# Attention scores from split queries and keys: three rounded products in place of one full-precision product, gammas moved ahead of the transposition, heads paired, the causal mask by selection

## The reference, cut to what matters

```python
x = _rmsnorm(tokens, norm_w)
q = (x @ Wq).reshape(b, n, QH, DH).transpose(0, 2, 1, 3)       # QH = 16 query heads of DH = 64
kv = x @ Wkv                                                    # H = 8 key and value heads
k = kv[..., :H * DH].reshape(b, n, H, DH).transpose(0, 2, 1, 3)
v = kv[..., H * DH:].reshape(b, n, H, DH).transpose(0, 2, 1, 3)
q = _mh_rmsnorm(q, q_gamma)                                     # l2norm(q) * (gamma + 1) * 8
k = _mh_rmsnorm(k, k_gamma)
q = q.reshape(b, H, g, n, DH)                                   # g = 2 query heads share a key head
sim = jnp.einsum('bhgid,bhjd->bhgij', q, k)
sim = jnp.tanh(sim / SOFTCLAMP) * SOFTCLAMP
sim = sim * DH ** (-0.5)
sim = jnp.where(causal, neg, sim)                               # token i sees tokens j <= i
attn = jax.nn.softmax(sim, axis=-1)
out = jnp.einsum('bhgij,bhjd->bhid', attn, v)                   # summed over g as well
return out.transpose(0, 2, 1, 3).reshape(b, n, H * DH) @ Wout
```

## Time and profile before

| | us |
|---|---|
| median of 3 runs | 2039.68 (2038.79 to 2041.76) |
| the profiled execution, its own time | 2037.89 |
| its span, first to last instruction | 2036.2 |
| PE busy, share of the span | 1841.0, 90% |
| DVE busy | 1184.6, 58% |
| ACT busy | 876.8, 43% |
| POOL busy | 473.1, 23% |

### The profile page before, as it was taken

The page is one execution under the profiler, slowest core; times in us unless marked ns, Lnnn a source line. Parts: engine busy times, 40 slices in busy tenths (PEclk is TensorE's granted clock), DMA queues, the critical chain, the costliest instruction groups (busy, mean ns, idle before and its releaser), DMA issues. The chain is left out here.

```text
span 2036.2 us, 31526 instructions
## 1 busy us (share of the span) xinstructions
PE 1841.0 (90%) x11768; PEld 1585.8 (78%) x11768; DVE 1184.6 (58%) x2083; ACT 876.8 (43%) x1076; POOL 473.1 (23%) x376
## 2 busy tenths in 40 slices
PE   3699999999969989998998999699999999999997
PEld 2698988988957877777787778578778787777876
DVE  6788788888865786776678676323241423414141
ACT  3655654545525764664576466122221222222221
POOL 2100000000022231221232123133433324333342
PEclk8799999999998999998999999799999999999999
DMA  8131222224001002000200100150000000000000
GB/s 168 49 128 49 96 78 90 76 99 143 22 32 63 23 15 77 24 15 9 85 23 15 56 22 22 49 223 14 8 21 0 21 0 21 21 0 21 0 11 12
DMA packets 17240, 96.81 MB, mean 48 GB/s; under 512 B 3270, under 2 KB 3398, under 8 KB 11209
## 3 DMA queue, kind: packets, MB, share of 16 engines
q1 hardware_dynamic: 17100, 94.90, 13.9%
HBM read 82.27 MB, written 24.15 MB: 52 GB/s over the span
## 5 line engine op out<-in xcount | busy, mean ns | idle before, releaser
L556 PE MATMUL conv<-w_hi,x_hi 128*128 128x368 f16 (+5 forms) x1320 | 355.8, 279 | 4.2 <-DVE planes L452 4.2
L556 PE MATMUL conv<-w_lo,x_hi 128*128 128x368 f16 (+5 forms) x1320 | 356.2, 279 | 0.0
L556 PE MATMUL conv<-w_hi,x_lo 128*128 128x368 f16 (+5 forms) x1320 | 355.0, 279 | 0.0
L818 POOL TENSOR_TENSOR probs<-probs,mask 128x512 f32<-128x512 f32 x128 | 166.8, 1303 | 444.1 <-ACT probs L892 444.1
L1310 ACT ACTIVATE raw_c<-ring,sh 128x512 f32<-128x512 f32 x128 | 88.2, 689 | 370.3 <-PE ring L1407 370.3
L1098 PE MATMUL mixed<-v,probs 128*128 128x65 f32 x1536 | 202.9, 283 | 41.5 <-DVE parts L978 41.5
L1098 PEld LDWEIGHTS mixed<-v,probs 128*128 128x128 f32 x1536 | 187.2, 197 | 56.8 <-issue 40.0
L1407 PE MATMUL ring<-ha_hi,wh 128*128 128x512 f32 x512 | 208.2, 407 | 16.9 <-POOL ha_lo L1272 16.9
L1272 POOL TENSOR_TENSOR ha_lo<-raw_c,ha_hi 128x512 fp32r<-128x512 f32 x128 | 165.0, 1289 | 210.1 <-DVE ha_hi L1322 210.1
L1407 PE MATMUL ring<-ha_lo,wh 128*128 128x512 f32 x512 | 205.4, 401 | 0.0
L1322 DVE CAST ha_hi<-raw_c 128x512 fp32r<-128x512 f32 x128 | 80.7, 631 | 212.9 <-ACT raw_c L1310 210.7
(11 more groups left out here) (148 smaller groups left out, 3563.7 us busy)
## 6 DMA issues: line engine op xcount, KB each, us to landing
xt<-x_columns_in SPq DMA_DIRECT2D x12, 1163.0 KB, 5.3
xp<-x_patches_in SPq DMA_DIRECT2D x12, 1152.0 KB, 5.2
hidden_words<-hidden_weights_in SPq DMA_DIRECT2D x8, 1408.0 KB, 8.2
words<-hidden_words SPq DMA_DIRECT2D x32, 352.0 KB, 3.1
wh<-hidden_words SPq DMA_DIRECT2D x2, 4096.0 KB, 21.1
tokens<-planes SPq DMA_DIRECT2D x4, 1024.0 KB, 3.9
lines<-tokens SPq DMA_DIRECT2D x4, 1024.0 KB, 5.4
h<-tokens SPq DMA_DIRECT2D x4, 1024.0 KB, 7.4
```

Source lines behind the costliest of these rows:

```text
L556: ins = pe.matmul(out, xs[:, c, RI - 1 - i:RI - 1 - i + NR, :, x].rearrange("p r g -> p (r g)"), w, start=(t == 0), stop=(t == len(terms) ...
L818: pool.tensor_tensor(diag, diag, both, ALU.mult).then_inc(s_mask, 1)
```

## The change

Queries and keys are each split into a high part, rounded to fp32r (the type in which the kernel's other split products run), and a low part, the rest. Each score product becomes three: high x high, low query x high key, high query x low key, accumulated in PSUM. ACT writes the high part while it copies the bank (`q_hi`, `k_hi`, L888 of the changed kernel), and DVE then subtracts it from the same bank to get the low part (L971), so a bank of transposed data is read by two engines one after the other.

Both gammas are multiplied into the query columns of `raw` ahead of the transposition, on DVE (L966), with `gamma` now 128 x 1024 and loaded so. The heads are regrouped by the host's order of Wq: one score step is now a pair of neighbouring key heads (one on partitions 0 to 63, the other on 64 to 127), with one query head of each. So keys are transposed as they are, once: three transposition jobs per token block in place of four, and `keys` is gone. The two steps of a pair leave their results in `o` (first step) and `parts` (second step), and one addition of 256 columns per pair takes the place of two of 128. POOL masks with two affine selections of 128 x 2 x 128 on `probs` itself in place of a multiplication by a mask tile. The gammas' staging buffer is `xp`, so SP waits with their load until the last split of `xp`.

```diff
-                    for dst, src in ((sh.norm_w, NW), (sh.gq, GQ), (sh.gamma, GK)):
-                        sp.dma_start(dst[:], src).then_inc(sh.s_small, 16)
+                    sp.wait_ge(s_lo, LAST + 2)
+                    for dst, src in ((sh.norm_w[:], NW), (gq, GQ), (sh.gamma[:], GK)):
+                        sp.dma_start(dst, src).then_inc(sh.s_small, 16)
...
-                dve.tensor_tensor(sh.gamma[:], sh.gamma[:], sh.gq[:], ALU.mult).then_inc(sh.s_gamma, 1)
+                dve.tensor_tensor(sh.gamma[:], sh.gamma[:], gq, ALU.mult).then_inc(sh.s_gamma, 1)
...
-    [("make", 11), ("make", 7), ("scale", 1)],
+    [("make", 7), ("scale", 1)],
     [("make", 12)],
-    [("make", 13), ("make", 14), ("make", 15)],
+    [("make", 13), ("make", 14)],
...
-        qt = sb("qt", [P, 2, HEADS, TOK])
-        kt = sb("kt", [P, 2, HEADS, TOK])
+        q_hi = sb("q_hi", [P, 2, HEADS, TOK], F32R)
+        q_lo = sb("q_lo", [P, 2, HEADS, TOK], F32R)
+        k_hi = sb("k_hi", [P, 2, EB, TOK], F32R)
+        k_lo = sb("k_lo", [P, 2, EB, TOK], F32R)
...
-                        pool.tensor_tensor(diag, diag, both, ALU.mult).then_inc(s_mask, 1)
+                        settle(pool, s_settle)
+                        for jb in range(2):
+                            diag = probs[:, n % 4, :, 2 * jb * P:(2 * jb + 1) * P]
+                            ins = pool.affine_select(out=diag, in_=diag, compare_op=ALU.is_ge, fill=0.0, base=0,
+                                                     pattern=[[0, 2], [1, P]], channel_multiplier=-1)
+                        ins.then_inc(s_mask, 1)
...
-                        dve.tensor_tensor(heads[:, 0:QH], heads[:, 0:QH], by[:, 0:QH].to_broadcast([P, QH, DH]), ALU.mult)
-                        for m in range(2):
-                            ins = dve.tensor_tensor(keys[:, tb, :, m], heads[:, QH:],
-                                                    by[:, QH:].to_broadcast([P, HEADS, DH]), ALU.mult)
-                        ins.then_inc(s_qn, 1)
+                        dve.tensor_tensor(heads, heads, by, ALU.mult).then_inc(s_scaled, 1)
+                        dve.wait_ge(s_scaled, image(g, step[1]) * 2 + tb + 1)
+                        dve.tensor_tensor(raw[:, tb, 0:KV], raw[:, tb, 0:KV], gamma[:], ALU.mult).then_inc(s_qn, 1)
...
-                        dve.tensor_tensor(kt[:, img % 2, 4 * r:4 * r + 4, P * tb:P * tb + P], bank, by,
-                                          ALU.mult).then_inc(s_emptied["keys"], 1)
+                        dve.wait_ge(s_qkhi, image(g, img) * 6 + 3 * tb + r + 1)
+                        dve.tensor_tensor(transposed(q_lo, k_lo, img, tb, r), bank,
+                                          transposed(q_hi, k_hi, img, tb, r).bitcast(F32), ALU.subtract)\
+                           .then_inc(s_emptied["queries" if r < 2 else "keys"], 1)
...
-                        dve.tensor_tensor(parts[:], got[:, :, :, 0:DH], rl[:].to_broadcast([P, 2, 2, DH]),
+                        pair = o[:, img % 2, :, 2 * (hd // 2):2 * (hd // 2) + 2]
+                        dve.tensor_tensor(parts[:] if hd % 2 else pair, got[:, :, :, 0:DH], rl[:].to_broadcast([P, 2, 2, DH]),
                                           ALU.mult).then_inc(s_mixread, 1)
-                        dve.wait_ge(s_mixread, g * NH + n + 2)
-                        dve.tensor_tensor(o[:, img % 2, :, hd], parts[:, :, 0], parts[:, :, 1],
-                                          ALU.add).then_inc(s_o, 1)
+                        if hd % 2:
+                            dve.wait_ge(s_mixread, g * NH + n + 2)
+                            dve.tensor_tensor(pair, pair, parts[:], ALU.add).then_inc(s_o, 1)
...
                         for jb in range(2):
-                            for m in range(2):
-                                rows = slice(DH * m, DH * m + DH)
-                                ins = pe.matmul(sim[:, n % 2, m, 2 * P * jb:2 * P * jb + P * (2 - jb)],
-                                                kt[rows, img % 2, hd, P * jb:P * jb + P],
-                                                qt[rows, img % 2, hd, P * jb:TOK], start=True, stop=True)
+                            for t, (k, q) in enumerate(((k_hi, q_hi), (k_hi, q_lo), (k_lo, q_hi))):
+                                for m in range(2):
+                                    rows = slice(DH * m, DH * m + DH)
+                                    ins = pe.matmul(sim[:, n % 2, m, 2 * P * jb:2 * P * jb + P * (2 - jb)],
+                                                    k[rows, img % 2, hd // 2, P * jb:P * jb + P],
+                                                    q[rows, img % 2, hd, P * jb:TOK], start=(t == 0), stop=(t == 2),
+                                                    skip_group_check=True)
```

More of the change, by code:

```diff
@@ L109, in token_stage @@
         xp = sb("xp", [P, XW])
+        gq = xp[:, 0:QH * DH]
         x_hi = sb("x_hi", [P, CHANNELS, NR + 4, GI, NC], F16)
@@ L601, in first_order @@
     order += [("make", 0, j) for j in (4, 5, 6)] + [("scale", 0, 0), ("sum", 0, 1), ("root", 0, 1)]
-    order += [("make", 0, j) for j in (3, 7, 8, 9, 10, 11)] + [("scale", 0, 1)]
-    return order + [("make", 0, j) for j in (12, 13, 14, 15)]
+    order += [("make", 0, j) for j in (3, 7, 8, 9, 10)] + [("scale", 0, 1)]
+    return order + [("make", 0, j) for j in (12, 13, 14)]
 def attention_order(last):
@@ L702, in attention_stage @@
         raw = sb("raw", [P, 2, QK])
-        keys = sb("keys", [P, 2, HEADS, 2, DH])
         rn = sb("rn", [P, 2, QK // DH])
@@ L743, in attention_stage @@
         s_rn = sem("b_rn")
+        s_scaled = sem("b_scaled")
         s_qn = sem("b_qn")
+        s_qkhi = sem("b_qkhi")
         s_score = sem("b_score")
@@ L765, in attention_stage, with transposed @@
         image = lambda g, img: g * GI + img
+        def transposed(q, k, img, tb, r):
+            heads = q[:, img % 2, 4 * r:4 * r + 4] if r < 2 else k[:, img % 2]
+            return heads[:, :, P * tb:P * tb + P]
         @block.sync
@@ L796, in _ @@
             pool.memset(v[:], 1.0).then_inc(s_const, 1)
[L797 to L801, removed]
             def emit(run, g):
@@ L878, in emit @@
                                 act.activation(squares[:, 0:QK], raw[:, tb], ACT.Square).then_inc(s_sq, 1)
-                        elif r < 2:
+                        else:
                             bank = read_out(run, g, step)
                             act.wait_ge(s_score, m * HEADS + 8)
-                            act.activation(qt[:, img % 2, 4 * r:4 * r + 4, P * (tb - 2):P * (tb - 1)],
-                                           bank.rearrange("p (h t) -> p h t", t=P), ACT.Copy)\
-                               .then_inc(s_emptied["queries"], 1)
+                            act.activation(transposed(q_hi, k_hi, img, tb - 2, r), bank.rearrange("p (h t) -> p h t", t=P),
+                                           ACT.Copy).then_inc(s_qkhi, 1)
                     elif kind == "score":
@@ L1066, in emit @@
                             for e in range(4):
-                                if r < 2:
-                                    c = (4 * r + e) * P
-                                    src = raw[:, tb, c:c + P]
-                                else:
-                                    src = keys[:, tb, 4 * (r - 2) + e].rearrange("p m d -> p (m d)")
-                                ins = pe.transpose(bank[:, e * P:(e + 1) * P], src, ident[:])
+                                c = (4 * r + e) * P
+                                ins = pe.transpose(bank[:, e * P:(e + 1) * P], raw[:, tb, c:c + P], ident[:])
                             ins.then_inc(s_job, 1)
@@ L1097, in emit @@
                                     at = P * (ib + jb)
-                                    ins = pe.matmul(out, probs[:, n % 4, m, at:at + P], v[:, img % 2, jb, hd],
+                                    ins = pe.matmul(out, probs[:, n % 4, m, at:at + P], v[:, img % 2, jb, 2 * (hd // 2) + m],
                                                     start=(jb == 0), stop=(jb == ib), skip_group_check=True)
@@ L1517, in per_unit, with paired @@
         return np.asarray(s).reshape(KH, P).T
+    def paired(q):
+        return q.reshape(-1, HEADS // 2, 2, 2, DH).transpose(0, 1, 3, 2, 4).reshape(-1, QH * DH)
     w = lambda a: np.asarray(a)
```

28 lines of the change are left out of this document (11 added, 17 removed).

## The result

The changed kernel takes 2028.3 us in the median of 15 runs (2019.7 to 2048.5) against 2041.4 for the kernel before (15 runs, 2034.8 to 2051.1): a ratio of 0.9945, 95% interval 0.9922 to 0.9969. It is 0.55% faster, where 0.3% was forecast. The profiled executions differ by 13.0 us (2024.89 against 2037.89), where the sum said 6.7. The changed kernel's runs lie further apart; the last experiments bear on that.

What follows compares the result with a forecast made beforehand. PE sets the pace by a small margin, with DVE right behind. Terms -3.6 - 2 - 2.8 + 1.4 + 0.3 = -6.7 from 2037.89 give 2031.2; the median, 1.8 higher, 2033 us, range 2022 to 2062 (forecast's own 2024 to 2041).

Steps and rivals of the forecast that it cites:

- POOL ... I take 0.9. The lock shortens by a third: POOL's mask: two selections of 256 columns take 0.8 to 1.2 us, taken as 0.9, against 1.30 now.
- The walk: One mid-group image followed step by step through the changed order; its net change was put at 0.
- Rival A: DVE's relief exceeds its new work and PE's saving arrives in full: 16 x 1.3 = -21, 2019 us; 8%.
- in such an image PE's 0.88 - 0.32 = 0.55 us turn into waits: 0: Mid-group image: PE's 0.88 us saved on transposes, less 0.32 for scores, becomes waiting, so no time is gained.
- Score step, 0.76 to 0.80: PE's score products before each mix: six split pairs take 0.80 us against 0.76, +5 us over 128 steps.
- Group ends -2.8, norm images -3.6, four images behind a projection -2, last image +0.3: Changes in us at three group ends, three images with next group's norms, four behind a group's projection, and the last image.
- First stretch +1.4, token stage 0: First stretch: DVE's serial chain lengthens, +1.4 us; token stage: larger gammas taken at 0, up to 2.7 us.
- B: PE's passes alone set the price: score steps save 15 to 20 us, transposes 14; 2016 us; 3%.
- C: Split products of 128 columns in each score step run at the fp32 price: 2060 to 2066 us; 13%.
- E: Halves of split products don't run side by side, six pairs become twelve in a row: +74, 2107 us; 3%.
- F: The change moves nothing, all gains are eaten: 2036 to 2042 us; 9%.
- D: ACT and DVE on each bank lengthen waits at job 12 and image's end by 0.7 to 1.6 us: 2042 to 2056; 22%.

Runs made afterwards that it cites:

- the last experiments: Steps moved around two TensorE standstills: kernel before with selections, 1998.9 us (0.9803); changed kernel with keys last and mix read first, 2004.7 us (0.9834).

## Why the prediction was right, and where its steps were off

The direction and the range held, and 2033 was 5 us off. That closeness is in part luck. It hides two errors that partly cancel: the mask's gain and the price of the rest were both sized too small. The stages show the same: the forecast left the mid-group images at 0 where they gave 3.3 us in all, and the first image took 4.6 us more where it should have gained.

- **"POOL ... I take 0.9. The lock shortens by a third"**: the term that was mis-sized. The time of a selection was nearly right (0.493 each in the mean), its worth was not. The walk let the second norm chain wait 0.5 us where it waits 0.23, and put the third mix's reading 0.3 to 0.4 us later where it is 0.3 earlier. Alone the mask is worth 1.4 us per mid-group image and 31 us in all, the clock's share included. Its cost showed in how long the one operation beside it was held, and at which place. (The lower bound of a selection, one column per ns on top of 0.294, is 0.42 and not 0.40; the median came out at 0.407.) The forecast had the 37 us of lock waits in hand and used them for Rival A only.
- **"in such an image PE's 0.88 - 0.32 = 0.55 us turn into waits: 0"**: it was -0.65. PE's busy time fell as forecast (0.49 for 0.55), but its idle time, which should have grown by as much, fell by 0.16. That TensorE's saving is mostly eaten is shown: putting the eight transposes back costs 0.3, not 0.88. The low part ahead of the reading and the wait at job 12 stood where the walk put them, with 0.9 and 0.6 us when each is removed.
- **Score step, 0.76 to 0.80**: the whole step, with the change-over to the next work, went from 0.85 to 0.83 or 0.84, not to 0.89. The 5 us charged for it in the walk (0.32 per image) were not there. Of the two gaps between the pairs of 128 columns, one is at the bound from below (half of 0.118), the other at the floor.
- **"-14 for the transposes"** as work holds; as time it was a third of that.
- **Group ends -2.8, norm images -3.6, four images behind a projection -2, last image +0.3**: measured -6.4, -4.0, +1.8 and -2.6. All four include stretches at the lower clock that differ between the two executions. The first image took 44.5 us at a mean clock of 0.74 in this one execution (39.9 at 0.90 before), and the terms had no room for that.
- **First stretch +1.4, token stage 0**: both as measured.
- **Rivals.** B, C and E fell by the score rows, F by the interval. D's places are job 12 and the image's end; TensorE waits 0.35 and 0.3 us there, far from its 0.7 to 1.6 more. But its kind of wait is real at a place that it doesn't name: with the mask by product the low part of job 8 helps to hold the fourth mix for 2.1 us, and the kernel is 38 us slower than before. The selections kept the change off that side. A is right that VectorE's relief outweighs its new work (TensorE idles 0.16 us less per image), but TensorE's saving did not arrive in full, and the additions it pointed to are worth nothing by themselves. A's price is also less than its own words add up to: 0.55 and most of 1.6 us is about 2 per image, not 1.3. The measured image, 35.4 us, lies between the forecast's sign (near 36.1) and A's (34 to 35).

What stays open: how the 18 us between the changed kernel and the mask alone divide between VectorE's places (0.7 us in each of 15 images is 10) and the clock, since the stretches at the lower clock differ from one kernel's profile to the other's.

## What to carry to other kernels

When one change has many parts, time the smallest part alone first: here a four-line mask outdid the whole. When GpSimd and VectorE work side by side on SBUF, count which VectorE operation is held and who waits behind it; shorter GpSimd instructions can help although nothing waits for GpSimd itself. And when two engines are nearly level, moving what the waiting engine doesn't need behind the read that it does need gave 1.0 us per mid-group image, as much as the low parts cost, though the time followed only when the standstills were moved too.

## What the runs showed of the hardware

- A selection over 128x256 takes 0.407 us in the median (two one behind the other 0.77), at the lower of the two bounds of the forecast, where a multiplication of 128x512 takes 1.28. It waits in its turn: two selections beside a scaling and the gammas (1.75 and 1.31 us) took 3.36 us.
- A standstill of TensorE of 1.15 to 1.33 us in the last image was followed by the lower clock level in four profiled executions and not in seven, at the same place of nearly the same program. Once fallen, the clock stayed at 0.50 for 41 to 44 us, through some 25 us of which TensorE was busy throughout. The last scores came about 10 us later for it, and the end 11 to 16.
- Of the three pairs of split products of 64 rows and 128 columns in a score step, the second starts 0.06 us behind the first and the third 0.11 behind the second.
